# The recurrent stage of a four-layer graph network written out, and its normalisation's apply done by ScalarE alone

## What is computed

```python
def _L2_gnn_ref(x, adj, mask, weight, w_ih, w_hh, b_ih, b_hh):
    A = (adj != 0).astype(x.dtype)
    h = x
    for l in range(weight.shape[0]):                # 5 steps
        m = jnp.einsum('bnd,de->bne', h, weight[l])
        agg = jnp.einsum('bij,bid->bjd', A, m)
        h = _gru_cell(agg, h, w_ih, w_hh, b_ih, b_hh)
    return h * mask[..., None]
...
x = _layernorm(x + _L0_gnn_ref(...), axis=-1)       # stage A
x = _layernorm(x + _L1_gnn_ref(...), axis=-1)       # stage A
x = _layernorm(x + _L2_gnn_ref(...), axis=-1)       # stage B, the recurrent stage
x = _layernorm(x + _L3_gnn_ref(...), axis=-1)       # stage C
```

## Time and profile before

| | |
|---|---|
| time, median of 3 runs | 1122.16 us (1120.86 to 1122.92) |
| the profiled execution's own time | 1123.02 us |
| its span (first to last instruction) | 1121.0 us |
| PE busy | 996.7 us, 89% |
| DVE busy | 887.8 us, 79% |
| POOL busy | 805.1 us, 72% |
| ACT busy | 796.7 us, 71% |
| mean granted TensorE clock | 0.946 |

### The profile page before, as it was taken

How to read it: one execution, slowest core, us unless ns; L and a number is a source line. 1 busy time by engine, 2 the same in 40 slices (tenths; PEclk the granted TensorE clock), 3 DMA queues, 4 the chain that set the end, 5 groups by cost and what they waited for, 6 DMA issues and landing times.

```text
span 1121.0 us, 21146 instructions
## 1 busy us (share of the span) xinstructions
PE 996.7 (89%) x6010; PEld 600.6 (54%) x6010; DVE 887.8 (79%) x2447; ACT 796.7 (71%) x1375; POOL 805.1 (72%) x879
## 2 busy tenths in 40 slices
PE   3699999395999999999998999999999999877884
PEld 2599998242345544444554554454455454466763
DVE  4599999464677888889898897887889977767895
ACT  1378888373678787887887878777788876736554
POOL 0589999374458888786796887887779777678353
PEclk9699999598999999999999999999999999988897
DMA  7133332224454444335425424433443543312323
GB/s 166 42 111 113 111 101 65 57 48 79 53 91 89 70 94 85 76 70 101 85 56 103 86 56 95 84 70 81 84 83 63 107 66 71 74 31 60 83 76 83
DMA packets 294971, 90.25 MB, mean 81 GB/s; under 512 B 222291, under 2 KB 294764, under 8 KB 294892
## 3 DMA queue, kind: packets, MB, share of 16 engines
q1 hardware_dynamic: 281066, 88.55, 36.9%
q10 hardware_dynamic: 13826, 0.85, 0.9%
HBM read 28.58 MB, written 8.81 MB: 33 GB/s over the span
## 4 chain that ended last, share of the span: by engine, by line
PE 53%; DVE 19%; issue 10%; POOL 8%; ACT 4%; DMA 2%; ACTq 2%; DVEq 0%; SPq 0%; POOLq 0%
PE psum L1277 14%; PE psum L1272 13%; PE psum L1273 13%; PE psum L1301 5%; DVE st L890 4%; POOL zh L637 3%; PE psum L1352 3%; DVE x L901 2%; DVE mv L894 2%; ACTq L758 2%; DVE ws L1037 2%; PE psum L1367 2%; DMA hnp<-htp 2%; DVE ot L1184 1%; DVE ws L1027 1%
## 5 line engine op out<-in xcount | busy, mean ns | idle before, releaser
L637 POOL TENSOR_TENSOR zh<-zw,ht 128x512 f32<-128x512 f32 x160 | 203.3, 1271 | 41.7 <-ACT zw L824 38.2
L596 POOL TENSOR_TENSOR htp<-ht,htp 128x512 f16<-128x512 f32 x128 | 148.1, 1157 | 87.6 <-ACT htp L785 87.4
L1272 PE MATMUL psum<-htp,wh_hi 128*128 128x512 f16 x480 | 184.0, 383 | 25.5 <-DMA htp<-hxp 14.7
L1272 PE MATMUL psum<-pth,wx_hi 128*128 128x512 f16 x480 | 184.9, 385 | 14.0 <-ACT pth L767 14.0
L1277 PE MATMUL psum<-ptl,wx_hi 128*128 128x512 f16 x480 | 184.1, 384 | 5.2 <-DVE ptl L1109 4.3
L1273 PE MATMUL psum<-pth,wx_lo 128*128 128x512 f16 x480 | 184.4, 384 | 0.0
L1277 PE MATMUL psum<-htp,wh_hi 128*128 128x512 f16 x480 | 183.9, 383 | 0.0
L1273 PE MATMUL psum<-htp,wh_lo 128*128 128x512 f16 x480 | 183.8, 383 | 0.0
L1083 DVE SCALAR_TENSOR_TENSOR rt<-psum,bhn,rt 128x512 f32<-128x512 f32 x160 | 119.8, 748 | 65.8 <-ACT rt L797 65.7
L824 ACT ACTIVATE zw<-psum,brz,unscale 128x512 f32<-128x512 f32 x160 | 124.1, 776 | 53.6 <-PE psum L1277 53.5
L1109 DVE SCALAR_TENSOR_TENSOR ptl<-psum,pth 128x512 f16<-128x512 f32 x160 | 110.2, 689 | 61.6 <-ACT pth L767 61.5
(11 more groups left out here) (170 smaller groups left out, 1955.0 us busy)
## 6 DMA issues: line engine op xcount, KB each, us to landing
adj<-in_adj_dram SPq DMA_DIRECT2D x32, 256.0 KB, 2.9
x<-in_x_dram SPq DMA_DIRECT2D x32, 256.0 KB, 3.3
adjr<-in_adj_dram SPq DMA_DIRECT2D x32, 256.0 KB, 3.1
out_dram<-yo SPq DMA_DIRECT2D x8, 768.0 KB
hnp<-htp SPq DMA_TRANSPOSE x128, 3.1
out_dram<-xq SPq DMA_DIRECT2D x32, 50.0 KB
v<-in_L_gnn_W_dram SPq DMA_DIRECT2D x2, 640.0 KB, 5.4
x3q<-x SPq DMA_DIRECT2D x16, 50.0 KB
```

Of the source, the lines that this page charges most:

```text
L596: nc.gpsimd.tensor_tensor(HT_LO[s % 2], HT[s][:, :], HT_HI[s % 2], ALU.subtract).then_inc(b_htl, 1)
L637: nc.gpsimd.tensor_tensor(ZH[s % 2][:, :], ZW[s % 2][:, :], HT[s][:, :], ALU.mult).then_inc(b_zh, 1)
L1272: mm(dst, w_h[:, col:col + P], h[:, :], start=start, stop=False)
```

## The change

1. `run_b` no longer makes a loop: rounds 1 to 6 are written out for all engines as rounds 0 and 7 were. The work and its order are those of the loop body; addresses and semaphore values become constants, and the jumps and register instructions are gone.
2. The apply of the normalisation for a group of stage B is done for all four graphs by ACT (`range(G4)`), at the place where it did two. The DVE block at lag 26 is gone, and so is the second semaphore: who waited for both halves waits for `b_x3`, now from ACT.

```diff
@@ -304,19 +304,14 @@
                 return None
             return j % TURN // STREAMS, j % STREAMS, at
 
-        def run_b(eng, slot, unrolled=False):
+        def run_b(slot):
 
             def body(it, slots):
                 for j in slots:
                     slot(lambda lag: item(j - lag, it))
             body(0, range(-EARLY, TURN))
-            body(1, range(TURN))
-            if unrolled:
-                for it in range(2, ROUNDS - 1):
-                    body(it, range(TURN))
-            else:
-                with eng.Fori(2, ROUNDS - 1) as it:
-                    body(it, range(TURN))
+            for it in range(1, ROUNDS - 1):
+                body(it, range(TURN))
             body(ROUNDS - 1, range(TURN + 4))
 
         def nth(x):
...
@@ -465,7 +460,6 @@
 
             def load_c(k):
                 sp.wait_ge(b_x3, (k + 1) * GC // G4)
-                sp.wait_ge(b_x3h, (k + 1) * GC // G4)
                 xv = x2[0:NODES, k * GC * D:(k + 1) * GC * D].rearrange("p (q t d) -> p q t d", t=G4, d=D)
                 for t in range(G4):
                     sp.dma_start(X3Q[k % 4][t * NODES:(t + 1) * NODES, :].rearrange("p (q d) -> p q d", d=D),
...
@@ -624,7 +618,6 @@
                     hi, lo = halves(FNP[s])
                     pool.wait_ge(b_tf[s % 2], turned_last(x))
                     reach(pool, b_x3, gth(x) - STREAMS)
-                    reach(pool, b_x3h, gth(x) - STREAMS)
                     nc.gpsimd.tensor_tensor(YB[s][:, :], hi, lo, ALU.add).then_inc(b_ye, 1)
                 x = at(2)
                 if x:
...
@@ -805,11 +798,11 @@
                 if x and x[0] == L - 1:
                     l, s, it = x
                     wait_apart(act, b_nm, gth(x))
-                    for i in range(G4 // 2):
+                    for i in range(G4):
                         last = nc.scalar.activation(
                             x2[:, bass.ds(it * (STREAMS * G4 * D) + (s * G4 + i) * D, D)], cols(YB[s], i),
                             ACT.Identity, bias=NMB[s][:, i:i + 1], scale=RSB[s][:, i:i + 1])
-                    last.then_inc(b_x3h, 1)
+                    last.then_inc(b_x3, 1)
                 x = at(-13)
                 if x and x[0] == 0 and x[1] < 2:
                     l, s, it = x
...
@@ -829,7 +822,7 @@
             act.wait_ge(w_v, W_BRZ)
             act.wait_ge(w_sc, W_SCALED + 2)
             act.wait_ge(a_x2, STEPS_A)
-            run_b(act, slot_b)
+            run_b(slot_b)
 
             def apply_c(k, some):
 
...
@@ -1045,15 +1038,6 @@
             run_a(dve, step_a)
 
             def slot_b(at):
-                x = at(26)
-                if x and x[0] == L - 1:
-                    l, s, it = x
-                    wait_apart(dve, b_rs, gth(x))
-                    for i in range(G4 // 2, G4):
-                        last = nc.vector.tensor_scalar(
-                            x2[:, bass.ds(it * (STREAMS * G4 * D) + (s * G4 + i) * D, D)], cols(YB[s], i),
-                            MVB[s][:, 2 * i:2 * i + 1], RSB[s][:, i:i + 1], ALU.subtract, ALU.mult)
-                    last.then_inc(b_x3, 1)
                 x = at(-1)
                 if x and x[0] == 0:
                     l, s, it = x
...
@@ -1145,7 +1129,6 @@
                 if has(0):
 
                     dve.wait_ge(b_x3, (k + 1) * GC // G4)
-                    dve.wait_ge(b_x3h, (k + 1) * GC // G4)
                     for i in range(GC):
                         last = nc.vector.bn_stats(STC[:, 6 * i:6 * i + 6], x2[:, (k * GC + i) * D:(k * GC + i + 1) * D])
                     last.then_inc(c_bs, 1)
```

More of the change, by code:

```diff
@@ L260, in graph_stack_kernel @@
         b_bs, b_mv, b_ve, b_rs, b_nm = sem("b_bs"), sem("b_mv"), sem("b_ve"), sem("b_rs"), sem("b_nm")
-        b_nmn, b_x3, b_x3h = sem("b_nmn"), sem("b_x3"), sem("b_x3h")
+        b_nmn, b_x3 = sem("b_nmn"), sem("b_x3")
         c_ldx = [sem(f"c_ldx{i}") for i in range(4)]
@@ L511, in slot_b @@
                     sp.dma_start_transpose(blocks(FNP[s]), FTP[p][:, :]).then_inc(b_tf[p], 16)
-            run_b(sp, slot_b, unrolled=True)
+            run_b(slot_b)
             for k in range(STEPS_C + 2):
@@ L648, in slot_b @@
                     nc.gpsimd.tensor_tensor(NMB[s][:, :], NMB[s][:, :], minus[:, 0:G4], ALU.mult).then_inc(b_nm, 1)
-            run_b(pool, slot_b)
+            run_b(slot_b)
             def step_c(k, has):
@@ L1118, in slot_b @@
                           .then_inc(b_sxl, 1)
-            run_b(dve, slot_b)
+            run_b(slot_b)
             def step_c(k, has):
@@ L1326, in _ @@
             pe.wait_ge(a_x2, STEPS_A)
-            run_b(pe, slot_b)
+            run_b(slot_b)
             def step_c(k, has):
```

## The result

The changed kernel takes **1113.9 us** (median of 4 runs, 1112.46 to 1116.15) against 1122.2 us for the kernel before beside it (1120.86 to 1122.92). The ratio is 0.9929, with a 95% interval of 0.991 to 0.9949. The kernel is faster by about 8.3 us where 4.3 were forecast: right sign, just inside the lower end of the range, and twice the size. Lines of the changed kernel have moved by some 5 to 17: the P pass stands at L1284, `hi_passes` at L1255 and L1256, ACT's apply at L802, `zw` at L817, `pth` at L760, DVE's f16 adjacency at L1046.

What follows compares the result with a forecast made beforehand. PE bounds stage B at 87 us a round, plus ACT's apply, the jump back and DVE's apply. Stage B 0.0 (-13.4 + 1.2 - 9.1 + 21.3) and stage C -4.3 from 1122.16 gave 1117.8 us, range about 1113.5 to 1122.

Steps and rivals of the forecast that it cites:

- The term of ACT's two more instructions: Stage B, four apply slots in each of rounds 1 to 7: 0.76 us more per slot, +21.3 us.
- the ring: Stage B apply slots: PE and ACT wait on each other through sigmoid r, apply, sigmoid z and `Z_B`; period 4.42 us.
- Rival D: ACT's two more instructions cost half because PE's ring has unseen slack: 10.7 us less, 1107.1 us; chance 0.10.
- The 1.51 us of slot 3: Stage B, rounds 2 to 7: DVE's apply, held until POOL's `ht` ends, costs PE 1.51 us per round; 9.1 us saved.
- Rival C: The DVE/POOL shut-out moves to another DVE instruction in stage B, so the 9.1 us stay: 1126.9 us; chance 0.05.
- Rival A: Clock falls after four idle times of PE in a row, 1.7 us lost per round: 1129.7 us, slower; chance 0.08.
- Jumps gone: Ends of rounds 2 to 5: without the jumps back, their excess over round 6 goes, saving 13.4 us.
- step 0: Start of stage C: without DVE's applies `yo` starts 1.9 us earlier, POOL's earlier end brings 1.2 more: -3.1 us.
- The fetches of straight code: Rounds 2 to 6 written out: new code costs 0.25 us a round, five times, +1.2 us, between 0 and 9.
- step 2: Stage C, ACT applies the last four groups: two more instructions for the last one in the chain, +0.8 us.
- step 3: Stage C: DVE's applies for four groups before `nmc` and `yo` go, -2.0 us.
- Rival B: No difference: new code costs 0.8 us a round and stage C's extra 1.2 us fails: 1121.7 us; chance 0.15.

Runs made afterwards that it cites:

- the kernel with the second part alone: The changed kernel with the loop over rounds 2 to 6 put back on PE, ACT, POOL and DVE: 1113.77 us, ratio 0.9929.
- the two kernels with a shorter stretch of lower clock: Kernel before with rounds 2 to 6 written out, DVE's apply kept: 1106.98 us; kernel before with 40 memsets at start of DVE's program: 1108.2 us.

## Why the prediction was right or wrong

**The end state was right.** "P passes 4.33 us apart in plain slots and 5.18 where ACT has its apply, with PE idle until `zw`; all rounds from 1 to 6 near 90 us" is what the profile shows: 4.33, 5.19, 0.69 us idle, 90.06 to 90.27. The term of ACT's two more instructions, 28 x 0.76, is right to 0.01 us a slot, because the ring in the earlier trace rows was already closed with two, so that each further instruction counts whole. Rival D (half of it) is out with that.

**The 1.51 us of slot 3** (9.1 in all) went as said, and nothing took their place: slot 3 is at 4.33 us in the changed kernel and in the kernel with the second part alone, and at 5.84 us wherever DVE's apply stays at lag 26. Rival C is out.

**Rival A, the clock**, is out too. Four idle times of 0.69 us, 4.5 us of work apart, left the granted clock at 1.0 from 282 to 927 us, as the 0.62 and 0.54 of the earlier trace rows had. What the prediction says of the clock behind a jump is wrong, though: "This comes four times" holds for DVE's stand, but PE's idle time was 0.91 us at the first jump, and the lower clock followed only the second and the fourth, after 1.98 and 1.99 us. At the third PE idled just as long and the clock stayed at 1.0 (timeline, and window behind it with PEclk 1.00):

```profile
688.73 0.39 PE L1272 MATMUL psum<-htp,wh_hi 128*128 128x512 f16 x1 [2.01 <-DVE rt L1083]
```

```profile
688.70:692.10 3.40, 2.83 (x13) 1.09 (x14) 2.94 (x6) 2.19 (x4) 0.78 (x1) 1.00 0.63 146
```

The sum didn't suffer, since it took the lengths of the rounds: 92.3 us for the two with the lower clock, 91.2 and 91.6 without.

**The reading that does not carry over is "Jumps gone": "All of that goes in principle: saving 13.4."** As a difference between the two kernels' rounds it is right, and so the sum held. As the worth of the part of the change that writes the rounds out, it is wrong beside the other part: removing the apply from DVE shortened its loop body by 20 instructions, and at that length and place the jump is free. I took the 3.21 us of the earlier trace rows for the price of a jump. It is the price of DVE's jump from this body at this place: 40 instructions further on it is zero, with the body untouched. The argument that registers and waits cost PE nothing, "round 6 less the 1.51 us equals round 1", was empty, since 1.51 was taken from just that difference; the kernel with only DVE written out supports it. The trace could have warned: PE, ACT and POOL jumped at the ends of the same rounds, and PE's idle time there had DVE named at its end, not its own "issue". The rule that I quoted there from the Trainium skill (Runtime: NRT & Kernel Launch, Instruction fetch mechanics), that a taken branch outside the window forces a fetch, agrees with these runs as far as it goes. Its blocks of 256 instructions don't: a shift by 128, half of such a block, brings the stand back as a shift by 256 does.

**Terms that were mis-sized.** The fetches of straight code: +1.2 us taken, 0.3 measured (0.2 in round 2, 0.06 in round 4), which is 0.9 us of the miss. The earlier trace rows were not the price of new code: with the second part alone round 2 is the first pass through a loop body too, and lasts 90.09 us, as the rounds behind it. Why the kernels that keep the loop and share the apply have some 0.5 to 0.7 us in round 2 (88.95 and 89.25 us without DVE's stand) stays open.

As ACT's slots came out 0.01 us longer 27 times, 0.6 us of it is left in rounds 1 to 7, which are 1.4 us shorter where 0.8 was forecast.

Behind the last P pass the forecast is -4.3 + 0.76 = -3.5 us and the profile says -5.3. By the intervals of `sp_t`: the fourth apply slot +0.8 as forecast; step 0 -3.1 and -1.6 where 1.9 and 1.2 were forecast. Set against the two kernels with a shorter stretch of lower clock (see above) it is 1.7 and at most 1.3, so the term of 3.1 us was about right; at least 1.7 us of the 4.7 is the clock's, which the forecast had only in its range ("some 2 us either way from where the lower clock falls"), and is luck. The rest: step 2 +0.8 as forecast; step 3 -1.7 where it said -2.0; later steps -0.4.

The two misses together make -4.3 - 0.6 - 1.8 = -6.7 us. The rest up to the measured 8.3 lies inside the interval of the ratio (5.7 to 10.1 us), and in the profiles it lies ahead of round 1, in code that didn't change. Rival B, no difference, would have been 1121.7 us, and its fetches didn't come. The prediction also counted three things that add to 87 us in a round and missed a fourth, round 7's wait of 2.4 us with the slow slot behind it; both kernels have it, so the difference stood.

**What stays open**: whether it is blocks of code that the stand fetches, and how many stay loaded; why the start of round 1 and the later steps of stage C move by 1 to 5 us between kernels that are the same there; and why the lower clock follows a wait of about 2 us in one place and not in another. No run took these apart.

## What to carry to other kernels

Two changes that each help can hold the same gain twice: measure each alone before adding them, and where one removes instructions from an engine, ask what that does to its code's place and length. A stand of 3 us for "issue" at a jump back is no property of loops; write out that one engine, or move its code by some tens of instructions, and look at the count of its instruction packets (53 with the stand, 33 without). Before moving an operation to an engine in a closed ring, look at whether it is slow by itself (340 ns) or only beside a neighbour (1299 ns): another slot on the old engine left the kernel 24 us faster than the move did (1090.2 against 1113.9).

## What the runs showed of the hardware

- A DVE jump back cost 2.8 to 3.2 us of DVE's time or nothing, decided by where in the engine's program the same 287 instructions lie: starts at 821, 949 and 1077 cost it, 861 does not. The jumps of PE, ACT and POOL cost nothing that reached PE in rounds 3 to 6 of any kernel of this case.
- The price on PE can be larger than the wait: in the kernel before, the rounds with a jump were 2.7 to 3.8 us longer than one without, with 0.9 to 2.0 us of idle time at once. The 3.8 are the two where 3.4 us at 1.2 GHz followed; after 2.01 us of idle time elsewhere none did. Idle times of 0.7 us, four in a row, brought no lower clock.
- A ring of two engines over one PSUM bank has room for 0.67 us of other work per slot here, and nothing beyond: one pair of applies costs 0.09 us, two pairs 0.86.
